# A state-space layer and an FP4 feed-forward network: early tiles read their columns in place, new instruction lists for the beginning, and unread products in the last three tiles

## The reference

```python
xB = einsum('bsh,nh->bsn', x, B);  xD = einsum('bsh,oh->bso', x, D)      # B 16 x 256, D 256 x 256
state_t = state_(t-1) @ A.T + xB_t                                       # A 16 x 16, scan over 2048 steps
ssm = layernorm(einsum('bsn,hn->bsh', states, C) + xD) * gamma + beta
x1  = layernorm(x + ssm)
q(v): blocks of 16; scale = max|v| / 6, values rounded to the grid 0, .5, 1, 1.5, 2, 3, 4, 6
h   = silu(q(x1) @ q(w_gate).T) * (q(x1) @ q(w_up).T)                    # w_gate, w_up 704 x 256
out = layernorm(x1 + q(h) @ q(w_down).T)                                 # w_down 256 x 704
```

## Time and profile before

| | |
|---|---|
| median of 3 runs | 596.43 us (595.5 to 598.21) |
| profiled execution | 600.9 us, of it span 598.3 us |
| TensorE busy | 556.8 us (93%), 3665 products and transposes |
| VectorE, GpSimd, ScalarE busy | 86%, 82%, 79% |
| mean granted TensorE clock | 0.947 of 2.4 GHz |
| moved by DMA | 38.33 MB |

### The profile page before, as it was taken

One profiled execution on the slowest core, in us unless ns is written; L12 is line 12 of the kernel. 1 busy time (PEld: TensorE's weight loads), 2 busy tenths in 40 slices (PEclk: granted clock), 3 DMA queues, 4 the chain that ended last, 5 costly groups with the idle time before them and its releaser, 6 DMA issues.

```text
span 598.3 us, 12712 instructions
## 1 busy us (share of the span) xinstructions
PE 556.8 (93%) x3665; PEld 495.7 (83%) x3665; DVE 513.0 (86%) x1228; ACT 472.4 (79%) x1422; POOL 493.2 (82%) x672
## 2 busy tenths in 40 slices
PE   7449949999999999999999999999999999999974
PEld 6346637799999999999999999999999999999863
DVE  5138536999999999999999999999999999999971
ACT  3245546688888888998888888888888888888753
POOL 2037346799999999999999999999999999998642
PEclk7757868999999999999999999999999999999996
DMA  8950011111111112111111111111111111100000
GB/s 292 408 123 2 7 50 49 39 41 47 57 58 58 58 48 60 54 56 55 51 53 56 56 56 56 56 56 56 56 56 56 56 56 55 53 21 18 19 27 35
DMA packets 38075, 38.33 MB, mean 64 GB/s; under 512 B 7008, under 2 KB 36768, under 8 KB 37024
## 3 DMA queue, kind: packets, MB, share of 16 engines
q1 hardware_dynamic: 38048, 38.00, 20.1%
HBM read 19.50 MB, written 8.39 MB: 47 GB/s over the span
## 4 chain that ended last, share of the span: by engine, by line
PE 80%; DVE 6%; SPq 6%; POOL 2%; DMA 2%; issue 2%; ACT 2%; POOLq 0%; DVEq 0%; ACTq 0%
PE gu L1331 39%; PE turned L1331 18%; PE yb L1331 7%; PE turned L1397 7%; PE turned L1357 2%; DMA xtTile<-xT 2%; SPq L394 1%; SPq L336 1%; PE yb L1345 1%; PE turned L1408 1%; PE turned L1407 1%; SPq L381 1%; DVE scratch L1026 1%; DVE scratch L1050 1%; DVE htLo L1055 1%
## 5 line engine op out<-in xcount | busy, mean ns | idle before, releaser
L1331 PE MATMUL gu<-wguHi,xtHi 128*128 128x512 f32 (+1 forms) x384 | 151.6, 395 | 1.4 <-DVE xtLo L1019 1.3
L1331 PE MATMUL gu<-wguLo,xtHi 128*128 128x512 f32 (+1 forms) x384 | 144.3, 376 | 0.0
L1331 PE MATMUL gu<-wguHi,xtLo 128*128 128x512 f32 (+1 forms) x384 | 144.3, 376 | 0.0
L1331 PE MATMUL turned<-wdHi,htHi 128*128 128x256 f32 x320 | 92.1, 288 | 3.8 <-DVE htLo L1055 3.8
L508 POOL TENSOR_TENSOR scratch<-scratch 128x704 f32<-128x704 f32 x64 | 92.1, 1440 | 2.9 <-DVE scratch L1040 2.2
L513 POOL TENSOR_TENSOR scratch<-scratch 128x640 f32<-128x640 f32 x64 | 82.0, 1281 | 12.1 <-DVE scratch L1050 12.1
L1331 PE MATMUL turned<-wdHi,htLo 128*128 128x256 f32 x320 | 91.6, 286 | 0.0
L1331 PE MATMUL turned<-wdLo,htHi 128*128 128x256 f32 x320 | 90.7, 283 | 0.0
L1331 PEld LDWEIGHTS gu<-wguHi,xtLo 128*128 128x128 f32 x384 | 72.5, 189 | 12.3
L1331 PEld LDWEIGHTS gu<-wguHi,xtHi 128*128 128x128 f32 x384 | 72.5, 189 | 11.1 <-DVE xtLo L1019 2.3
L1331 PEld LDWEIGHTS gu<-wguLo,xtHi 128*128 128x128 f32 x384 | 72.7, 189 | 8.2
(11 more groups left out here) (194 smaller groups left out, 1622.2 us busy)
## 6 DMA issues: line engine op xcount, KB each, us to landing
xT<-in_L_attn_x_dram SPq DMA_DIRECT2D x8, 1024.0 KB, 13.4
xtTile<-xT SPq DMA_DIRECT2D x64, 128.0 KB, 2.1
scratch<-in_L_attn_x_dram SPq DMA_DIRECT2D x64, 128.0 KB, 2.4
out_dram<-scratch SPq DMA_DIRECT2D x64, 128.0 KB, 1.9
stTile<-statesHi SPq DMA_DIRECT2D x128, 8.0 KB, 1.7
stTile<-statesLo SPq DMA_DIRECT2D x64, 8.0 KB, 1.7
scratch<-in_L_ffn_w_down_dram SPq DMA_DIRECT2D x1, 704.0 KB, 14.1
scratch<-in_L_ffn_w_up_dram SPq DMA_DIRECT2D x1, 640.0 KB, 12.8
```

The costliest lines, as they stand in the source:

```text
L1331: ins = nc.tensor.matmul(to, l, r, start=(first and q == 0), stop=(last and q == len(passes) - 1))
```

## The change

1. **Early columns.** For tiles 0 to 15 t_hi and t_lo read xT itself. load_columns does nothing for them.
2. **SyncE's list.** tMat, cStack and qPad go out between the weights and the x pieces; the x rows of tiles 0 to 3, gamma and beta come after the last x piece; the x rows of tiles 4 to 7 come ahead of all states. The steps are then split in load_columns, load_states and load_tile.
3. **New lists** for TensorE, ScalarE, VectorE and GpSimd up to the `run` calls. VectorE copies eleven groups of turned x and no longer two. Five busy(1) stand between the powers.
4. **The end.** The down projections of the last five tiles go to yb, the bank of layer, and h_turn no longer waits for add_x1 of such a tile. In the last three tiles TensorE gets batches of four unread products: ahead of ffn_down for tiles 61, 62 and 63 and ahead of h_turn for tiles 62 and 63, 20 products in all.

```diff
-    VECTOR_COPIES = (0, 28)
+    VECTOR_COPIES = (0, 2, 7, 9, 14, 15, 17, 19, 23, 25, 28)
-    FILLED = dict(pe=7, act=8, dve=6, pool=8)
+    FILLED = dict(pe=7, act=8, dve=6, pool=8, sp=8)
+        TAIL = 5
+        def is_late(h, m):
+            return isinstance(h, int) and h * CHUNK + m >= TILES - TAIL
+        def down_bank(h, m):
+            return yb[:, 0:H] if is_late(h, m) else db
+        def is_early(h, m):
+            return isinstance(h, int) and h * CHUNK + m < PEELED * CHUNK
+        def tile_columns(h, m):
+            if is_early(h, m):
+                return xT[:, h, m, :, :]
+            return xtTile[:, m % RING, :, :]
...
             load_x(2)
             load_x(3)
-            sp.dma_start(wg[:, full + 1:WG_ROWS, :],
-                         w_up[P - part:FF, :].rearrange("(r p) k -> p r k", p=P)).then_inc(s_wload[2], 16)
-            sp.dma_start(wX[:, WG_ROWS * H:].rearrange("p (r k) -> p r k", k=FF),
-                         w_down.rearrange("(r p) k -> p r k", p=P)).then_inc(s_wload[3], 16)
-            for h in range(4, HALVES):
-                load_x(h)
-            sp.dma_start(gamma_b[:, :], gamma.unsqueeze(0).to_broadcast([P, H])).then_inc(s_bcast, 16)
-            sp.dma_start(beta_b[:, :], beta.unsqueeze(0).to_broadcast([P, H])).then_inc(s_bcast, 16)
             sp.wait_ge(s_tDiag, 1)
             sp.wait_ge(s_pwc, POWER_COPIES[LOG_C + 1])
             for i in range(2, CHUNK, 2):
                 sp.dma_start(tMat[N * i:N * i + N, 0:N * i],
...
+            sp.dma_start(wg[:, full + 1:WG_ROWS, :],
+                         w_up[P - part:FF, :].rearrange("(r p) k -> p r k", p=P)).then_inc(s_wload[2], 16)
+            sp.dma_start(wX[:, WG_ROWS * H:].rearrange("p (r k) -> p r k", k=FF),
+                         w_down.rearrange("(r p) k -> p r k", p=P)).then_inc(s_wload[3], 16)
             sp.wait_ge(s_dDone, 2)
             sp.wait_ge(s_pad, 1)
             for q, part_ in enumerate((cHi, cLo, cHi)):
...
+            load_x(4)
+            load_x(5)
             sp.wait_ge(s_qpad0, 1)
             for c in range(SUPER):
                 r = SUPER - 1 - c
                 sp.dma_start(qPad[N * r:N * r + N, c // 4, c % 4, :],
...
+            load_x(6)
+            load_x(7)
+            for tile in range(RING):
+                sp.dma_start(xTile[:, tile, :], x_v[0, :, tile, :]).then_inc(s_ldx[tile], 16)
+            sp.dma_start(gamma_b[:, :], gamma.unsqueeze(0).to_broadcast([P, H])).then_inc(s_bcast, 16)
+            sp.dma_start(beta_b[:, :], beta.unsqueeze(0).to_broadcast([P, H])).then_inc(s_bcast, 16)
             def load_columns(h, m):
+                if isinstance(h, int) and h * CHUNK + m < PEELED * CHUNK:
+                    return
+                sp.wait_ge(s_y, done(h, m - RING))
-            copied(sp, 3)
-            for tile in range(RING):
-                load_columns(0, tile)
-            for tile in range(RING):
-                sp.dma_start(xTile[:, tile, :], x_v[0, :, tile, :]).then_inc(s_ldx[tile], 16)
...
-            def load(h, m):
...
+            load_tile(0, 4)
...
+            load_tile(0, 7)
+            load_states(0, 0)
...
+            load_states(0, 7)
-            run(sp, [(load, 0), (store, 12)], RING)
+            run(sp, [(load_columns, 0), (load_states, 0), (load_tile, 0), (store, 12)], FILLED["sp"])
...
             def t_lo(h, m):
-                nc.gpsimd.tensor_tensor(tLo[:, m % 2, :, :], xtTile[:, m % RING, :, :], as_f32(tHi[:, m % 2, :, :]),
+                nc.gpsimd.tensor_tensor(tLo[:, m % 2, :, :], tile_columns(h, m), as_f32(tHi[:, m % 2, :, :]),
             def t_hi(h, m):
-                act.wait_ge(s_ldt[r], done_dma(h, m))
-                nc.scalar.copy(tHi[:, m % 2, :, :], xtTile[:, r, :, :]).then_inc(s_thi, 1)
+                if is_early(h, m):
+                    copied(act, 4 * h + m // 2)
+                else:
+                    act.wait_ge(s_ldt[m % RING], done_dma(h - PEELED, m))
+                nc.scalar.copy(tHi[:, m % 2, :, :], tile_columns(h, m)).then_inc(s_thi, 1)
...
+            def is_last(h, m):
+                return isinstance(h, int) and h * CHUNK + m >= TILES - 3
+            def unread(to):
+                for _ in range(4):
+                    nc.tensor.matmul(to[:, 0:P], ident[:, :], ident[:, :], start=True, stop=True)
             def h_turn(h, m):
+                if is_last(h, m) and tile >= TILES - 2:
+                    pe.wait_ge(s_silu, TILES)
+                    unread(gu)
                 pe.wait_ge(s_qh, done(h, m))
                     pe.wait_ge(s_lo, done(h, m - 1))
-                    pe.wait_ge(s_r, done(h, m - 1))
+                    if not is_late(h, m - 1):
+                        pe.wait_ge(s_r, done(h, m - 1))
             def ffn_down(h, m):
-                pe.wait_ge(s_lo, done(h, m))
+                to = down_bank(h, m)
+                if is_late(h, m):
+                    pe.wait_ge(s_x1p, TILES)
+                    if is_late(h, m - 1):
+                        pe.wait_ge(s_r, done(h, m - 1))
+                if is_last(h, m):
+                    unread(to)
+                pe.wait_ge(s_lo, done(h, m))
```

More of the change, by code:

```diff
@@ L401, in _ @@
-            sp.wait_ge(s_sthi, 1)
-            load_states(0, 0, (0, 1))
-            sp.wait_ge(s_states, 1)
-            load_states(0, 0, (2,))
-            for tile in range(1, RING):
-                load_states(0, tile)
-            def load(h, m):
-                j, r = m % CHUNK, m % RING
-                tile = h * CHUNK + m
-                sp.wait_ge(s_y, done(h, m - RING))
-                sp.wait_ge(s_xb, done(h, m - RING))
-                load_columns(h, m)
+                if not isinstance(tile, int) or tile >= RING:
+                    sp.wait_ge(s_y, done(h, m - RING))
@@ L414, in load, with load_tile @@
                 if isinstance(tile, int) and tile == PEELED * CHUNK - 1:
                     sp.wait_ge(s_states, PAIRS)
-                load_states(h, m)
+                for q, part_ in enumerate((statesHi, statesHi, statesLo)):
+                    if isinstance(tile, int) and tile == 0 and q % 2 == 0:
+                        sp.wait_ge(s_states if q else s_sthi, 1)
+                    sp.dma_start(as_f32(stTile[N * q:N * q + N, r, :]), as_f32(part_[rows, cols])).then_inc(s_ld[r], 16)
+            def load_tile(h, m):
+                j, r = m % CHUNK, m % RING
+                sp.wait_ge(s_xb, done(h, m - RING))
@@ L565, in _ @@
             pow2(0, 3)
+            t_lo(0, 6)
             pow1(0, 4)
@@ L749, in _ @@
             powers(3)
+            g_copy()
+            xt_copy(1)
             powers(4)
-            xt_copy(1)
+            t_hi(0, 0)
             powers(5)
-            g_copy()
-            xt_copy(2)
+            t_hi(0, 1)
             xt_copy(3)
@@ L759, in _ @@
             powers(7)
+            xt_copy(6)
             w_abs(0)
-            xt_copy(6)
-            xt_copy(7)
             powers(8)
-            t_hi(0, 0)
-            t_hi(0, 1)
+            powers(9)
+            w_abs(1)
+            powers(10)
             xt_copy(8)
-            xt_copy(9)
-            w_abs(1)
             xt_copy(10)
             xt_copy(11)
-            powers(9)
-            w_hi(0)
             xt_copy(12)
             xt_copy(13)
-            powers(10)
-            xt_copy(14)
@@ L1068, in _ @@
             w_max(0)
+            xt_copy(2)
             w_recip(0)
@@ L1071, in _ @@
             w_recip(1)
+            xt_copy(7)
             w_sum(0)
@@ L1074, in _ @@
             w_sum(1)
+            xt_copy(9)
             w_grid(1)
             w_max(2)
+            w_recip(2)
+            xt_copy(14)
+            xt_copy(15)
+            w_sum(2)
+            w_grid(2)
             w_lo(0)
-            w_recip(2)
             w_max(3)
@@ L1117, in _ @@
             x_scale(0, 0)
+            w_lo(7)
             x_recip(0, 0)
+            w_lo(8)
+            x_sum(0, 0)
+            x_grid(0, 0)
+            w_lo(9)
             link(1, 0)
-            link(1, 1)
-            x_sum(0, 0)
-            link(1, 2)
-            x_grid(0, 0)
-            x_max(0, 1)
-            scale_gamma(0, 2)
-            x_scale(0, 1)
-            add_x(0, 2)
-            x_recip(0, 1)
-            link(1, 3)
-            x_lo(0, 0)
+            scale_gamma(0, 2)
+            x_max(0, 1)
+            add_x(0, 2)
+            x_scale(0, 1)
+            x_lo(0, 0)
+            x_recip(0, 1)
+            link(1, 1)
             x_sum(0, 1)
             x_grid(0, 1)
-            link(1, 4)
+            link(1, 2)
             scale_gamma(0, 3)
@@ L1414, in _ @@
             powers(0)
+            busy(1)
             powers(1)
+            busy(1)
             powers(2)
+            busy(1)
             powers(3)
-            powers(4)
+            busy(1)
+            g_products()
             x_transposes(0)
             x_transposes(1)
+            powers(4)
+            busy(1)
             powers(5)
```

(19 more changed lines are left out.)

271 lines of the change are left out of this document (135 added, 136 removed).

## The result

The changed kernel takes 574.33 us (median of four runs, 572.11 to 576.95) beside 597.32 for the kernel before (four runs, 595.5 to 600.17): ratio 0.9613, 95% interval 0.9549 to 0.9676. The forecast was 569.5 with a range of 560 to 581. The profiled execution took 576.95, with a span of 575.2 and 1.75 around it. Of the six runs of the changed kernel that were made later, one, 577.08, counts as slow (over 1.5% above the fastest of the six), and their ratio leaves it out.

A forecast was written before the change was run, and what follows sets the result against it. TensorE alone bounds the middle at 7.60 us per tile, unchanged; waits at the start and the end give -15.7 - 4.8 - 2.5 - 1.5 - 2.7 = -27.2. From 600.9 that is 573.7, times 0.9926 = 569.5 us, range 560 to 581.

The forecast's parts named there:

- The stall, 15.7: Beginning: with early columns ScalarE no longer waits in t_hi, so TensorE's wait for turned x goes: -15.7 us.
- The x loads, 4.8: Ahead of layer(0,2): x rows of tiles 4 to 7 issued before the states remove TensorE's idle time: -4.8 us.
- the clock, 2.5: From layer(0,2) to the first gate product: without the idle time TensorE regains part of its clock: -2.5 us.
- The new lists, 1.5: Beginning: reordered work fills gaps in the first tiles' chain, against nine more VectorE copies: -1.5 us.
- The tail, 2.7: Last tiles: unread products hold the clock and late projections use another bank: -2.7 us net.
- The -0.45: Tail: h_turn(63) no longer waits for add_x1(62) and starts when GpSimd's scale ends: -0.45 us.
- the +0.3: Tail: cost of the unread products, which delay h_turn(62) and the down projection of tile 61: +0.3 us.
- Rival 1: Beginning: lists better than allowed, waits shrink to VectorE's own work, all upper bounds reached: 561 us; chance 0.18.
- Rival 2: Beginning: transposes keep the clock at 0.5 throughout, costing 10 us: 579.5 us; chance 0.20.
- Rival 3: Beginning: the stall only moves to another late thing for ScalarE or VectorE: 583 up to 590 us; chance 0.08.
- Rival 4: SyncE's queue: 20 issues ahead of the last x piece hold it full; at 5.36 us each about 640; chance 0.03.
- The signs: Expected traces: no xtTile wait, no TensorE wait over 3 us after 22, layer(0,0) near 52, 7.60 per tile, tail clock 1.00.

The follow-up runs named there:

- the old lists: Kernel before with early columns and the change's whole SyncE list, but the other four engines' old lists and the old end: 575.61 us, ratio 0.9629.
- the old bank: Changed kernel with its 20 unread products, but all down projections in db and h_turn waiting for add_x1 again: 572.44 us, ratio 0.9573.
- the last version: Changed kernel plus nine unread products among the links, eight more busy(1) and three unread products ahead of x_turn(0,0) and layer(0,3): 568.22 us, ratio 0.9527.
- the x rows back: Changed kernel, but the x rows of tiles 4 to 7 each come behind the states of their tile again: 577.35 us, ratio 0.9669.

## Why the prediction was right

**The stall, 15.7: right in size, too simple in its course.** Early columns 8.4 and the queue's front 7.1 make 15.5. That this falls so near is in part luck: each step has 3 us or more to either side. Firmer is the sum of columns, x rows and queue's front, 0.0371 x 597.5 = 22.2 us (20.4 to 24.0), where 15.7 + 4.8 + 2.5 = 23.0 was forecast. But what the first removes is not the whole: tMat was late next (3.59 and 4.24 us), and only SyncE's new front, which issues the copies from 10.06 on, the first with 8.0 us to landing, gives that back. I had the tMat row before me and used it only to show a full queue, not as a wait in line. The trace shows 3.6 to 4.2 of the 7.1 as that wait; the rest is not isolated. The cause, too, is narrower than I put it: t_hi in a later place gave 12.6 us with every copy kept. The place of the last x piece held as forecast: issued at 21.57, and none of its transposes waits for it (the last group waits 0.35 us, for a ScalarE copy).

**The x loads, 4.8, and the clock, 2.5: right.** Together 7.3 forecast, 6.6 measured by ratios. In the traces layer(0,0) came 16.7 earlier and layer(0,2) 21.6: 4.9 between them.

**The new lists, 1.5: not found.** This is the term that the runs bear out least: 0.957 for the old lists with the old end's price taken off and 0.9576 for the new. With 3.5 us to either side the 1.5 itself is not ruled out; the bounds of 6 gained and 6 lost are. Of link(0,8), which starts 65.10 - 43.97 = 21.1 us earlier than before, the old lists have most already: with them it starts at 48.33 and layer(0,0) at 54.06. The lists bring link(0,8) forward by 4 us more, and of that nothing is left at layer(0,0) in the first profile and 3.2 us in the second. Why nothing of it reaches the time is open. It is not that the new lists lose more clock: over all runs they have 16.4 us of cold time and the old lists 30.4, of which the old end has some 10 (55.0 before, 44.4 with the new end alone).

**The tail, 2.7: right in the trace (2.8).** The clock held (1.00 in all windows from 555 to 569), h_turn(63) took the 0.87 forecast, the last projection 2.34 where about 2.1 was said. The -0.45 that I gave to the other bank is not its own: with the unread products the old bank did as well (11.28), without them the new bank still has 12.85 for 14.08. The two parts overlap, and the products alone bring all of the 2.8, the bank alone 0.9 to 1.2 (the old end's second trace, that of the old lists, has 13.77). Of the +0.3 that I gave as the products' price 0.06 can be seen: h_turn(62) starts 4.39 us after VectorE's last step L1065 before it, and 4.33 without the products. Measured in time the tail is 3.5, with 0.5 around the span.

**The sum.** By ratios 8.4 + 7.1 + 6.6 + 3.5 + 0 = 25.6 of 597.5 where 27.2 x 0.9926 = 27.0 was forecast, and in the first comparison 0.0387 x 597.5 = 23.1, known to 3.8 us either way. Up to 1.5 of the difference are the lists'. The other 2 to 3 are within what a run's own clock does to it, and the 1.5 lost ahead of the first down projection and 0.8 over the middle tiles are in them; I named neither.

**The rivals.** Rival 1 (561) did not come, and full clock would not have made it: the last version, with nearly no cold time, takes 568. Rival 2, the cold beginning, came in part. It is not a beginning at 0.5 throughout: some 16 us are cold, and at 0.42 each they cost 7, not 10 on top of the forecast, since before, 54 were cold. The Trainium skill, page "TensorE: Matmul & The Clock Gate", section "Part 4: PE-mode transpose", says that the full clock does not come on for transposes. This case's traces don't bear that out for transposes mixed with thin products: between 17.4 and 41.3 us the changed kernel stayed at 1.00 with them, and in the kernel before the clock rose at 43.0 behind five us of transposes with two powers among them. What speaks for it is the stretch from 41.3 to 51.5, where the same kind of mixture ran at 0.50 for ten us. No run has transposes alone for long. Rival 3, the moved stall, happened in the experiment with the columns alone, for 3.6 us. Rival 4 did not: the 20 issues from 10.06 on to the last x piece, out by 23.67, cost 0.7 us each, and the longest later group 5.61 / 4 = 1.4.

**The signs.** ScalarE has no wait for xtTile, and TensorE none over 1.4 us after 22 us. layer(0,0) came at 54.14 (52 was said) and the first gate product at 68.59 (67); 7.61 us per tile and the clock in the tail held.

## What to carry to other kernels

When a long wait is taken away, look up everything else that lands in the stretch it covered: here three copies of 2 to 6 KB were the next wait, and the row of one of them had been in plain sight. Before you change how data reaches an operation, try the operation later in its list; here a move of four lines gave at least as much as the new source. Once the long waits are gone, look at busy share and granted clock by the microsecond: here gaps of 0.4 to 0.9 us were followed by three to ten us at 1.2 GHz, and with a few unread products in the gaps the mean cold time went from 16.4 to 6.1 us and the time down by some 3, a gain not yet clear of the noise. And judge a step by several runs: one profile each, before and after, put the early columns at 15.5 us where the ratio has 8.4.

## What the runs showed of the hardware

The clock fell to 1.2 GHz behind two microseconds with a busy share of 0.28 and 0.35 and then stayed there for ten us (41.3 to 51.5) in which TensorE was busy throughout, with links of 64 columns and pair sums of 32 rows among transposes. In two other profiles of the same list it fell at the same place (41.0 and 39.3) and was back after 3.5 us (at 44.4 and 42.8). With nine fp32 products of 128x128 in the gaps it did not fall there, in two profiles of two. Not every gap does it: the window of 19 to 20 us has 0.34 and no fall behind it. And the fall at 10.6 came with TensorE busy for 0.98 to 1.00 of each microsecond from 2 on, in powers of 16x16 with the unread products of busy(1) between them; in two other profiles with the same list (the old bank, the x rows back) that fall did not come at all.

The same program lost more in some runs than in others: four profiles with the same beginning have their first gate product at 68.59, 68.78, 65.59 and 62.89 us. The differences of 2 us that a single profile shows there prove nothing about an edit. In the last version, where little clock was lost, four of six runs lie within 0.9 us (567.51 to 568.39).
